# Routed rows sent unscaled, blank rows written behind each expert, and two shared pairs behind the row tiles

## What is computed

```python
x = x + conv(layernorm(x)); x = x + ffn(layernorm(x))
x = x + attention(layernorm(x)); x = x + ffn(layernorm(x))

def ffn(x):                                  # x: 4096 x 128, E = 8 experts, I = 256
    logits = x @ gate_w
    top_val = max(logits); top_id = argmax(logits)
    xs = x * sigmoid(top_val)                # the score scales the row, ahead of the expert
    y = (silu(xs @ rt_gate[e]) * (xs @ rt_up[e])) @ rt_down[e]     # for e = top_id alone
    shared = (silu(x @ sh_gate) * (x @ sh_up)) @ sh_down
    return shared + y
```

## Time and profile before

| | us |
|---|---|
| median of 3 runs | 540.97 |
| lowest and highest | 538.65, 541.30 |
| the profiled execution | 543.39 |
| its span on the core | 541.7 |
| convolution, and the start of gating | 0 to 126 |
| gating and shared expert, MoE layer 0 | 126 to 178 |
| row tiles, layer 0 | 178 to 241 |
| attention | 248 to 391 |
| gating and shared expert, layer 1 | 391 to 458 |
| row tiles, layer 1 | 458 to 521 |
| routed rows back, and the output | 521 to 541.7 |

### The profile page before, as it was taken

The page is one execution under the profiler, slowest core; times in us unless marked ns, Lnnn a source line. Parts: engine busy times, 40 slices in busy tenths (PEclk is TensorE's granted clock), DMA queues, the critical chain, the costliest instruction groups (busy, mean ns, idle before and its releaser), DMA issues.

```text
span 541.7 us, 14203 instructions
## 1 busy us (share of the span) xinstructions
PE 468.0 (86%) x4428; PEld 359.0 (66%) x4428; DVE 368.3 (68%) x1178; ACT 260.7 (48%) x671; POOL 342.9 (63%) x458
## 2 busy tenths in 40 slices
PE   3989999882999899993899999998686998999980
PEld 1668878771765799972566666666464665999960
DVE  6598999695776656643767778777475767666533
ACT  3553455023453355543776766766333452555530
POOL 4554676355886266661998888888566884466640
PEclk9999999998899999997999999999786999999995
DMA  8999999991111233315000000000000111333228
GB/s 277 323 225 185 190 177 189 185 163 35 45 46 46 66 88 90 92 48 160 2 2 2 3 2 2 4 1 3 1 12 31 41 45 51 84 86 91 79 74 271
DMA packets 49671, 47.66 MB, mean 88 GB/s; under 512 B 4186, under 2 KB 45019, under 8 KB 49470
## 3 DMA queue, kind: packets, MB, share of 16 engines
q1 hardware_dynamic: 44320, 35.90, 31.1%
q0 software_dynamic: 4544, 9.35, 5.1%
q10 hardware_dynamic: 734, 1.50, 0.8%
HBM read 17.86 MB, written 28.87 MB: 86 GB/s over the span
## 4 chain that ended last, share of the span: by engine, by line
PE 71%; DVE 7%; issue 6%; ACT 5%; POOL 5%; DMA 3%; SPq 1%; DVEq 0%; ACTq 0%; POOLq 0%
PE bank L781 65%; PE bank L297 2%; PE bank L861 2%; PE bank L791 1%; DMA scores_odd<-routed 1%; ACT scores_odd L1188 1%; DMA residual<-x 1%; ACT wide L1188 1%; DMA routed<-row_out,row_token 1%; ACT k_tok L1188 1%; POOL sorted_rows L648 1%; PE bank L1136 1%; POOL routed L660 1%; POOL spect_y L692 1%; DVE prod L1533 1%
## 5 line engine op out<-in xcount | busy, mean ns | idle before, releaser
L660 POOL DMA_INDIRECT routed<-row_out,row_token x78 | 74.7, 958 | 65.3 <-DVE row_token L1575 49.5
L781 PE MATMUL bank<-row_in_t,row_weights 128*128 128x128 f32 x624 | 83.7, 277 | 1.3 <-issue 1.0
L648 POOL DMA_INDIRECT sorted_rows<-rows,place x64 | 62.8, 981 | 25.7 <-issue 12.5
L781 PEld LDWEIGHTS bank<-row_in_t,row_weights 128*128 128x128 f32 x624 | 75.7, 191 | 3.0 <-issue 2.5
L781 PE MATMUL bank<-wide,weights_sb 128*128 128x512 f32 x128 | 60.7, 613 | 0.4 <-DVE residual L1813 0.4
L1567 DVE TENSOR_SCALAR row_weights<-experts 128x512 f32 x78 | 34.0, 436 | 27.6 <-issue 24.0
L1232 ACT ACTIVATE row_silu<-bank 128x256 f32<-128x256 f32 x78 | 29.9, 384 | 47.0 <-PE bank L781 45.8
L1188 ACT ACTIVATE wide<-bank 128x512 f32<-128x512 f32 x56 | 30.6, 593 | 44.9 <-PE bank L791 28.3
L781 PE MATMUL bank<-experts,row_act 128*128 x312 | 49.4, 282 | 0.0
L1559 DVE TENSOR_TENSOR row_act<-row_silu,bank 128x256 f32<-128x256 f32 x78 | 32.7, 420 | 20.1 <-ACT row_silu L1232 11.3
L781 PE MATMUL bank<-normed_t,weights_sb 128*128 128x256 f32 (+1 forms) x112 | 41.4, 500 | 0.9 <-ACT normed_t L1188 0.9
(11 more groups left out here) (184 smaller groups left out, 1067.7 us busy)
## 6 DMA issues: line engine op xcount, KB each, us to landing
sorted_rows<-zeros SPq DMA_DIRECT2D x1, 17028.0 KB, 101.2
row_in<-sorted_rows SPq DMA_DIRECT2D x78, 64.5 KB, 1.9
rows<-routed SPq DMA_DIRECT2D x8, 256.0 KB, 4.9
scores_odd<-routed SPq DMA_DIRECT2D x8, 256.0 KB, 5.8
out<-residual SPq DMA_DIRECT2D x8, 256.0 KB, 4.6
routed<-row_out,row_token POOLq DMA_INDIRECT x78
tables_sb<-tables SPq DMA_DIRECT2D x1, 1024.0 KB, 9.1
experts<-rt_gate SPq DMA_DIRECT2D x1, 1024.0 KB, 18.7
```

The lines of the kernel that those rows point to most:

```text
L648: pool.indirect_dma_start(sorted_rows, bass.IndirectOffsetOnAxis(ap=place[:, t:t + 1].bitcast(U32), axis=0), rows[:, t, :], None).then_inc ...
L660: pool.indirect_dma_start(routed, bass.IndirectOffsetOnAxis(ap=row_token[:, r:r + 1].bitcast(U32), axis=0), row_out[:, r, :], None).then_i ...
L781: return pe.matmul(out_, lhsT, rhs, start=start, stop=stop, **kw)
```

## The change

The rows are sent unscaled. DVE's `apply_kept` writes the normed rows of all 32 tiles straight into `rows`, ACT computes the score as 0.5 tanh(top/2) + 0.5 (`score`, two activations of 128x4) into one more column of `rows`, and DVE scales each row tile by that column once it is loaded (`row_scale`), four tiles ahead. POOL's exp, DVE's two score rows and ACT's scaling are gone, and so are the waits of `apply_kept` for buffers. In place of the fill of `sorted_rows`, SP writes in each MoE layer, as soon as the counts are known, a tile of zeros behind each of seven experts' rows and eight tiles behind the last one's (`blank_ends`); row loads wait for these. `SHARED_LATER` goes from (1, 1) to (2, 2). `blank_table` moves from `row_tiles` into step 6.

```diff
-REGION = TILES * P
-SORTED = -(-((E - 1) * REGION + RT * P) // (8 * P)) * 8 * P
-BLANK_N = 2 * (D + 1)
+REGION = (TILES + 1) * P
+LAST_BLANK = E
+SORTED = (E - 1) * REGION + (TILES + LAST_BLANK) * P
+ROW = D + 2
+BLANK_N = 2 * ROW
-SHARED_LATER = (1, 1)
+SHARED_LATER = (2, 2)
...
+        def blank_ends(sp, m):
+            sp.wait_ge(e_tiles, tabled_to("blank_start", m))
+            for e in range(E):
+                tiles = LAST_BLANK if e == E - 1 else 1
+                start = sp.value_load(blank_start[0:1, e:e + 1], min_val=0, max_val=SORTED - tiles * P)
+                behind = sorted_rows[bass.ds(start, tiles * P), :]
+                if tiles > 1:
+                    behind = behind.rearrange("(p a r) d -> p a (r d)", p=P, r=2)
+                    sp.dma_start(behind, zeros.unsqueeze(1).to_broadcast([P, tiles // 2, BLANK_N])).then_inc(blanked, 16)
+                else:
+                    sp.dma_start(behind, zeros[:, 0:ROW]).then_inc(blanked, 16)
...
         def routed_io(sp, m):
+            blank_ends(sp, m)
             sp.wait_ge(e_tiles, tabled_to("tile_base", m))
             sp.wait_ge(e_sent, 16 * TILES * (m + 1))
+            sp.wait_ge(blanked, 16 * E * (m + 1))
...
-            clear_sorted(sp)
...
-            def exp_minus_top(k):
-                K = PAIRS * m + k
-                pool.wait_ge(e_route, routed_to("top", m, k))
-                wait(pool, e_score, 2 * (K - 1))
-                pool.tensor_tensor(exp_top[:, K % 2, :], inv_e[:], top[:, K % 2, :], ALU.pow).then_inc(e_exp, 1)
             def send_rows(k):
                 pool.wait_ge(e_route, routed_to("place", m, k))
+                pool.wait_ge(e_normed, PAIR * (PAIRS * m + k + 1))
+                pool.wait_ge(e_scored, PAIRS * m + k + 1)
                 if k == 0 and m == 0:
-                    pool.wait_ge(sorted_cleared, 16)
                     pool.wait_ge(tokens_numbered, 1)
                 for j in range(PAIR):
                     t = k * PAIR + j
-                    pool.wait_ge(e_rows, TILES * m + t + 1)
...
             def row_turn(n):
                 r, N = slot(m, n), RT * m + n
-                pe.wait_ge(row_loaded[r], 16 * (uses(m, n) + 1))
+                pe.wait_ge(row_scaled, N + 1)
...
-                    up_half(PAIRS - 1, 0)
+                    up_half(PAIRS - SHARED_LATER[m], 0)
...
                 pe.wait_ge(row_acted, RT * (m + 1))
-                up_half(PAIRS - 1, 1)
-                down(PAIRS - 1)
+                for k in range(PAIRS - SHARED_LATER[m], PAIRS):
+                    up_half(k, 1)
+                    if k + 1 < PAIRS:
+                        up_half(k + 1, 0)
+                    down(k)
...
+            def score(k):
+                K = PAIRS * m + k
+                act.wait_ge(e_route, routed_to("top", m, k))
+                act.activation(tangent[:, K % 2, :], top[:, K % 2, :], ACT.Tanh, scale=0.5).then_inc(e_tangent, 1)
+                act.wait_ge(e_tangent, K + 1)
+                act.activation(rows[:, k * PAIR:(k + 1) * PAIR, D + 1], tangent[:, K % 2, :], ACT.Identity,
+                               bias=half_col[:], scale=0.5).then_inc(e_scored, 1)
...
+            def row_scale(n):
+                r, N = slot(m, n), RT * m + n
+                dve.wait_ge(row_loaded[r], 16 * (uses(m, n) + 1))
+                dve.tensor_scalar(row_in[:, r, 0:D], row_in[:, r, 0:D], row_in[:, r, D + 1:D + 2], None, ALU.mult
+                                  ).then_inc(row_scaled, 1)
...
-                blank_table()
-                pipelined([(3, lambda i, r: row_expert(i) if i >= WEIGHT_BUFS else None), (2, each(row_gate_up)),
+                pipelined([(4, each(row_scale)), (3, lambda i, r: row_expert(i) if i >= WEIGHT_BUFS else None), (2, each(row_gate_up)),
                            (2, each(row_numbers))], RT)
```

More of the change, by code:

```diff
@@ L371, in hybrid_block @@
         act_sh = prod[:].rearrange("p (r i) t -> p r i t", r=2)
-        normed_of = (normed, *(conv_xv[:, c, :].rearrange("p (j d) -> p j d", j=PAIR) for c in range(2)))
         turn_bank = bank[0]
@@ L790, in turn @@
                 for j in range(PAIR):
-                    last = pe.transpose(turn_bank[:, j * P:(j + 1) * P], normed_of[k % NORMED_BUFS][:, j, :], ident)
+                    last = pe.transpose(turn_bank[:, j * P:(j + 1) * P], rows[:, k * PAIR + j, 0:D], ident)
                 last.then_inc(e_turned, 1)
@@ L1242, in row_tiles @@
                 shared_later(m, shared_silu)
-            return silu_table, keep, scale_rows, silu_half, step, row_tiles
+            return silu_table, keep, score, silu_half, step, row_tiles
         @block.scalar
@@ L1404, in third_keep @@
                 keep(2)
-                scale_rows(0)
+                score(0)
                 silu_half(0, 0)
@@ L1553, in step @@
                         row_expert(tile)
+                    blank_table()
             def row_gate_up(n):
```

99 lines of the change are left out of this document (39 added, 60 removed).

## The result

The changed kernel takes 549.23 us (median; 546.77 to 550.61), the kernel before, timed beside it, 539.81 us (538.57 to 541.30). The ratio is 1.0168, with a 95% interval of 1.0118 to 1.0219: slower by 9.4 us. The profiled execution of the changed kernel took 548.79 us, with a span of 547.1 us.

A forecast was written before the change was run, and what follows sets the result against it. PE, with 71% of the chain that ended last, plus its waiting gaps bounds the kernel. Terms -8.3 - 4.6 + 12.4 + 6.6 + 3.7 + 1.5 = +11.3 on the median 540.97 give 552.3 us; 8-in-10 range 543 to 561.

The forecast's parts named there:

- gating, layer 0: Start of gating in layer 0: fill, exp and scaling gone shorten PE's gap and the matmuls behind it, -8.3 us.
- gating, layer 1: Gating in layer 1: the exp wait goes and part of the same clock effect comes, -4.6 us.
- fronts, with the cold first tiles: In front of the row tiles: blank DMAs delay the first row load, PE returns at a lower clock; +6.2 us twice, +12.4.
- scaling in the row tiles: DVE's scaling of each row tile lengthens the two-tile loop, +0.085 us a tile over 39 tiles, twice: +6.6 us.
- second pair, layer 0, and the end: Second shared pair behind the row tiles: +3.7 us in layer 0 and +1.5 us at the end of the kernel.
- the first paragraph's: Reading of the timeline at layer 0's gating: POOL's 5.68 us idle before its first row DMA is the fill's wait.
- the 1.4 counted for the clock: Start of gating, layer 0: the 16 matmuls behind PE's gap run at 2.29 us or less, not 3.62.
- rival 2: Row tiles: DVE swallows the scaling in its 0.26 us idle a tile, so 545.7 us; chance 0.15.
- At nothing: Parts counted as costing nothing: tanh and extra column on ACT, `blank_table` in step 6, 520-byte rows, the fill's traffic.

## Why the prediction came out as it did

The forecast was 552.3, slower; measured 549.23, slower. The sign and the main cost were read rightly. That the sum came so near was in part luck: two terms were off by about 6 us each, in opposite directions. Measured against both profiles of the kernel before:

| term | forecast | against the earlier trace rows | against the second profile |
|---|---|---|---|
| gating, layer 0 | -8.3 | -7.3 | -2.4 |
| gating, layer 1 | -4.6 | -5.4 | -5.5 |
| fronts, with the cold first tiles | +12.4 | +13.5 | +13.4 |
| scaling in the row tiles | +6.6 | +0.7 | +0.7 |
| second pair, layer 0, and the end | +5.2 | +3.9 | +4.5 |
| sum (of the unrounded terms) | +11.3 | +5.4 | +10.6 |

(The fronts are 4.8 and 4.65 longer, and the first tiles to the fifth transpose 2.5 and 1.5; the rest of the row tiles' stretch is the term for the scaling.)

**Gating, layer 0.** Right against the profile that was read, and wrong as a statement on the kernel. The step that failed is the first paragraph's: 5.68 us of POOL's wait for the fill was taken for a property of the kernel, and it was one of that execution. The sum was then set against the median by taking off 2.4, as if that execution were longer everywhere; it was longer at the very place that the change removes, by 4.3. Of the 1.4 counted for the clock 0.5 came (3.62 to 3.15). The numbers hinted at the fill: a fill that lands at 124.9 where the row DMA is otherwise due at 119, in an execution 2.4 above the median.

**Gating, layer 1.** Near in size, -5.4 for -4.6, but the cause was wrong. The exp had been named; by the run with tanh alone it gives 1.4 at most, none of it between the first `chosen_b` matmul and `n_tok`. There the changed kernel is 3.8 faster, and the rest of the 5.4 lies ahead, with the clock. Between kernels that share this stretch it takes 189.8 to 193.1, so the size is no firmer than 3 us.

**Fronts.** Right step by step: blank DMAs 1.13 apart (1.11 forecast), the large one landing 4.1 behind its issue (4.6), the first row load 14.06 behind `n_tok` (14.5), PE idle 10.95 (11). Only the cold clock was too cheap: 2.5 and 1.5 in the first tiles, not 1.3 each. One thing the prediction didn't see: the row load wasn't all that the old front waited for. In the second profile it stands 8.22 behind `n_tok`, not 9.78, and the front is 13.32 all the same, since PE's second transpose then waits 1.70 for the add of pair 6, which the change moves away. The Trainium skill, "DMA: Bandwidth & Descriptors", section on latency and other measured facts, has about 600 ns as the floor of a register load. Here 1.13 less the issue of 0.33 leaves 0.80: the floor isn't undercut, and it isn't the price.

**Scaling in the row tiles.** This is the step that was wrong: rival 2, which had 0.15, is what happened. The prediction said that the scaling "can't hide in the register load, since that begins when the row ahead has ended". The rows of DVE with none, one and two scalings show the opposite: the load goes on beside them. Also the duration, 353 ns by the nearest row, is 280; that row had two per-partition scalars, this one has one. The Trainium skill, "VectorE: DVE Perf Modes", section on the TRN2 errata, has the formula behind the prediction's estimate of 127 ns and says itself that it under-predicts a single operation; the 280 ns here agree with that. Rival 2's time, 545.7, did not come, since its sum still held the gain of the fill's wait.

**Second pair.** Right in layer 0, 3.6 for 3.7. (Two halves of 1.88 and down matmuls of 2.29 are 6.05, not 5.9; it doesn't matter here.) At the end of the kernel 1.5 was forecast and 0.3 or 1.1 measured. Nothing is idle between the last shared add and the first routed add, as forecast.

**"At nothing".** `blank_table` in step 6 is free only as long as the blank rows are late. That was not said in the prediction, and the table costs 1.65 us in layer 1 as soon as they are gone.

The two large errors nearly cancel, which is luck and no part of the working. With the fill's wait left out and the scaling at 0.7, the same working gives 11.3 + 4.3 - 5.9 = +9.7 against an execution without that wait, where +9.4 was measured.

## What to carry to other kernels

A fill that runs early beside other work is cheaper than writing exactly the rows that are needed if their addresses are known only at the last moment: eight register loads and DMAs in a row stood between counts and rows, and cost 9 us here, to save a transfer of 17 MB that one of two profiled executions did not wait for at all. Before a wait in a profile is turned into a gain, ask whether it stands in a second execution, above all where a long transfer ends close to its first reader. And an operation of 0.28 us put in front of a register load, even two of them, can be nearly free, so the idle time marked "issue" in front of the load's user is room and not only loss. Last, a median that agrees with a sum does not bear out its terms; the stretches between events that both kernels have do that.

## What the runs showed of the hardware

- A register load on DVE runs beside the work queued ahead of it: the idle time in front of its user was 0.35, 0.20 and 0 us with none, one and two operations of 0.28 us in between.
- The fill's time goes by the piece. 17.0 MB in pieces of 1032 bytes landed 101.2 and 90.4 us after the issue in two executions, in pieces of 4128 bytes 50.6; 17.7 MB in pieces of 1040 bytes 70.7, of 4160 bytes 52.0, 51.9 and 52.2. That 1040 bytes are so much better than 1032 I had not expected; one profile shows it and nothing here says why.
- A short idle time of PE cost it the clock. After 4.81, 5.51 and 10.95 us it came back at a granted 0.50. After 4.56 us its first transpose still took 0.30, and the matmuls 1.4 us later ran at 0.50. After 3.15 us (layer 1 of the same kernel) the granted clock was 1.00 for another 2 us and then 0.51, with PE at work. The first row tiles took 4.8 to 6.0 us in all these cases, 3.4 in the kernel before, and not less after the shorter idle times.
